# Norm shifts moved from VectorE to GpSimd, weight splitting moved from GpSimd to ScalarE and VectorE, and orders changed in a four-layer graph network

## Time and profile before

| | |
|---|---|
| median of three runs | 1450.76 us |
| the profiled execution, its own time | 1449.63 us |
| its span in the trace | 1447.8 us |
| TensorE busy | 1393.4 us, 96% |
| ScalarE busy | 1297.7 us, 90% |
| VectorE busy | 1235.4 us, 85% |
| GpSimd busy | 973.2 us, 67% |
| data moved | 39.74 MB, mean 27 GB/s |

### The profile page before, as it was taken

How to read it: one execution, slowest core, us unless ns; L and a number is a source line. 1 busy time by engine, 2 the same in 40 slices (tenths; PEclk the granted TensorE clock), 3 DMA queues, 4 the chain that set the end, 5 groups by cost and what they waited for, 6 DMA issues and landing times.

```text
span 1447.8 us, 45196 instructions
## 1 busy us (share of the span) xinstructions
PE 1393.4 (96%) x14088; PEld 1321.1 (91%) x14088; DVE 1235.4 (85%) x5648; ACT 1297.7 (90%) x4166; POOL 973.2 (67%) x1299
## 2 busy tenths in 40 slices
PE   5899999999999999999999999999999999999996
PEld 4799999999999999999999999999999999999985
DVE  3788889889889888888888888898898898898885
ACT  4899999999999999999999999999999999999973
POOL 4567667667667667667667667667667667667652
PEclk9999999999999999999999999999999999999998
DMA  3000000100001000101000001000101000101000
GB/s 113 17 17 16 24 21 26 31 20 28 31 19 29 31 18 31 31 17 31 31 17 31 31 17 31 31 17 31 31 17 31 31 17 31 31 16 38 16 23 31
DMA packets 38109, 39.74 MB, mean 27 GB/s; under 512 B 2416, under 2 KB 37488, under 8 KB 37872
## 3 DMA queue, kind: packets, MB, share of 16 engines
q1 hardware_dynamic: 37872, 36.84, 8.4%
HBM read 20.05 MB, written 16.78 MB: 25 GB/s over the span
## 4 chain that ended last, share of the span: by engine, by line
POOL 40%; DVE 30%; issue 20%; PE 7%; ACT 2%; SPq 1%; DVEq 0%; POOLq 0%; DMA 0%; ACTq 0%
DVE masked L751 10%; POOL rstd L952 7%; POOL h_t_lo L972 7%; DVE stats L741 6%; POOL probs L979 4%; POOL probs L1010 4%; POOL probs L960 4%; POOL probs L976 4%; POOL inv_norm L965 3%; POOL xb L1008 3%; PE mid L321 3%; DVE shift L814 3%; DVE y_t_lo L806 2%; POOL rel_sq L1004 2%; DVE neg_max L751 2%
## 5 line engine op out<-in xcount | busy, mean ns | idle before, releaser
L562 ACT ACTIVATE probs<-masked,neg_max 128x128 f32<-128x128 f32 x1024 | 396.7, 396 | 0.0
L952 POOL TENSOR_TENSOR rstd<-var_eps,minus_half 128x2 f32<-128x2 f32 x320 | 245.2, 766 | 25.1
L751 DVE CUSTOM_DVE_ANT_0 masked<-mid,mask 128x128 f32<-128x128 f32 x1024 | 234.0, 283 | 2.3 <-issue 2.2
L1004 POOL TENSOR_TENSOR rel_sq<-rel 128x256 f32<-128x256 f32 x64 | 39.3, 613 | 264.2 <-DVE rel L844 264.2
L562 ACT ACTIVATION_READ_ACCUMULATOR probs<-masked,neg_max 128x1 f32 x1024 | 200.1, 195 | 0.0
L356 PE MATMUL bank<-ident,probs 128*128 128x128 f32 x1024 | 143.4, 273 | 0.5 <-POOL probs L979 0.5
L741 DVE BATCH_NORM_STATS2 stats<-x 128x6 f32<-128x256 f32 x384 | 138.8, 403 | 3.8 <-DMA x<-in_x 3.5
L766 DVE SCALAR_TENSOR_TENSOR h_t_lo<-bank,h_t_hi 128x512 fp32r<-128x512 f32 x64 | 44.3, 691 | 105.3 <-ACT h_t_hi L644 105.3
L356 PEld LDWEIGHTS bank<-ident,probs 128*128 128x128 f32 x1024 | 115.9, 141 | 1.3 <-POOL probs L979 0.8
L644 ACT ACTIVATE h_t_hi<-bank 128x512 fp32r<-128x512 f32 x64 | 38.2, 597 | 80.0 <-PE mid L321 78.7
L972 POOL TENSOR_TENSOR h_t_lo<-h_t_full,h_t_hi 128x512 fp32r<-128x512 f32 x64 | 108.1, 1689 | 0.8 <-ACT h_t_full L660 0.8
(11 more groups left out here) (160 smaller groups left out, 5991.2 us busy)
## 6 DMA issues: line engine op xcount, KB each, us to landing
x<-in_x SPq DMA_DIRECT2D x64, 256.0 KB, 3.0
out_x<-x SPq DMA_DIRECT2D x64, 256.0 KB, 3.2
w_qkv_sb<-in_w_qkv SPq DMA_DIRECT2D x1, 768.0 KB, 5.0
w_v_sb<-in_w_v_t SPq DMA_DIRECT2D x1, 256.0 KB, 5.3
w_proj_sb<-in_w_proj SPq DMA_DIRECT2D x1, 256.0 KB, 5.5
w_q_sb<-in_w_q SPq DMA_DIRECT2D x1, 256.0 KB, 6.1
w_k_sb<-in_w_k SPq DMA_DIRECT2D x1, 256.0 KB, 6.5
w_gat_x<-in_w_gat SPq DMA_DIRECT2D x1, 256.0 KB, 6.1
```

Source lines behind the costliest of these rows:

```text
L562: last = act.activation(probs[:, r, s], masked[:, r, s], ACT.Exp, scale=-1.0, bias=neg_max[:, r, s:s + 1], accum_out=sums[:, r, s:s + 1])
L751: last = dve.tensor_tensor_reduce(out=masked[:, r, s], in0=mid[:, r, s * N:(s + 1) * N], in1=mask[:], scale=1.0, scalar=LARGE, op0=ALU.add ...
L952: pool.tensor_tensor(rstd[:, k], var_eps[:, k], minus_half[:], ALU.pow).then_inc(ln_rstd[k], 1)
```

## The change

1. All four shifts leave VectorE. GpSimd makes them right after rstd, in `inverse_root_and_shift`: it first makes the negated mean (one more 128x2 operation) and then the product (another).
2. The hi parts of `SPLIT` and `LATE_SPLIT` are made by ScalarE (start of its steps 1 and 2), the lo parts by VectorE (start of its steps 2 and 3). GpSimd keeps only the two sums of biases.
3. The fold moves from step 2 to step 3 on TensorE and ScalarE, its low part on VectorE from step 3 to 4; VectorE's `last_constants` (with beta_ident and wa_prod) from step 2 to 3.
4. On ScalarE the copy of v1 moves from between the exponentials of groups 3 and 2 to between h_t_hi of norm 0 (L644) and h_t_hi of norm 2 (L648).
5. On VectorE the inverse of the sums of groups 2 and 3 moves behind x4, and x3_up waits also for an earlier h3.

The diff, cut to its core:

```diff
@@ pe @@
             def fold():
-                pe.wait_ge(max_ready[0], done(0, 1))
+                pe.wait_ge(max_ready[0], done(1, 1))
...
             def next_weights():
-                pe.wait_ge(split_ready, 2 * len(SPLIT))
+                pe.wait_ge(split_lo_ready, len(SPLIT))
...
-            run(pe, step, [(0, first_weights), (1, value_weights), (2, fold), (4, folded_weights),
+            run(pe, step, [(0, first_weights), (1, value_weights), (3, fold), (4, folded_weights),
                           (2, next_weights), (6, last_weights)])
@@ act @@
+            def next_constants():
+                act.wait_ge(const_in, 16 * len(CONSTS))
+                for w, (hi, _) in SPLIT:
+                    act.activation(hi[:], w, ACT.Copy).then_inc(split_ready, 1)
+
+            def last_constants():
+                act.wait_ge(late_const_in, 16 * len(LATE_CONSTS))
+                for w, (hi, _) in LATE_SPLIT:
+                    act.activation(hi[:], w, ACT.Copy).then_inc(late_split_ready, 1)
...
                     exps(3).then_inc(probs_ready[3], 1)
-                if on[4]:
-                    act.wait_ge(v1_psum, done(p4))
-                    wait_before(act, rel_v_psum, p4)
-                    act.activation(v1[:].rearrange("p b d -> p (b d)"), v1_bank, ACT.Copy).then_inc(v1_ready, 1)
-                if on[1]:
                     act.wait_ge(max_ready[2], done(p1))
...
                     act.activation(flat(h_t[0][0]), z0_bank, ACT.Relu).then_inc(h_hi_ready[0], 1)
+                if on[4]:
+                    act.wait_ge(v1_psum, done(p4))
+                    wait_before(act, rel_v_psum, p4)
+                    act.activation(v1[:].rearrange("p b d -> p (b d)"), v1_bank, ACT.Copy).then_inc(v1_ready, 1)
                 if on[5]:
                     act.wait_ge(h_t_psum[2], done(p5))
...
-            run(act, step, [(0, first_weights), (2, copy_fold)])
+            run(act, step, [(0, first_weights), (3, copy_fold), (1, next_constants), (2, last_constants)])
@@ dve @@
             def next_constants():
                 dve.wait_ge(const_in, 16 * len(CONSTS))
+                for j, (w, (hi, lo)) in enumerate(SPLIT):
+                    dve.wait_ge(split_ready, j + 1)
+                    dve.tensor_tensor(lo[:], w, hi[:].bitcast(f32), ALU.subtract).then_inc(split_lo_ready, 1)
 
             def last_constants():
                 dve.wait_ge(late_const_in, 16 * len(LATE_CONSTS))
+                for j, (w, (hi, lo)) in enumerate(LATE_SPLIT):
+                    dve.wait_ge(late_split_ready, j + 1)
+                    dve.tensor_tensor(lo[:], w, hi[:].bitcast(f32), ALU.subtract).then_inc(late_split_lo_ready, 1)
...
+            moments_read = [shift_ready[0], shift_ready[1], shift_ready[2], shift3_ready, ln_rstd[4]]
+
             def moments(k, p, src):
-                wait_before(dve, ln_rstd[k], p)
+                wait_before(dve, moments_read[k], p)
...
-                if on[6]:
-                    dve.wait_ge(ln_rstd[2], done(p6))
-                    wait_before(dve, z_ready[2], p6)
-                    dve.scalar_tensor_tensor(shift[2][:], mean_var[:, 2, :, 0], -1.0, rstd[:, 2], ALU.mult, ALU.mult)\
-                       .then_inc(shift_ready[2], 1)
...
-            run(dve, step, [(1, first_constants), (3, fold_low), (2, next_constants), (2, last_constants)])
+            run(dve, step, [(1, first_constants), (4, fold_low), (2, next_constants), (3, last_constants)])
@@ pool @@
             def last_constants():
...
-                for w, (hi, _) in LATE_SPLIT:
-                    pool.tensor_copy(hi[:], w).then_inc(late_split_ready, 1)
-                pool.wait_ge(late_split_ready, len(LATE_SPLIT))
-                for w, (hi, lo) in LATE_SPLIT:
-                    pool.tensor_tensor(lo[:], w, hi[:].bitcast(f32), ALU.subtract).then_inc(late_split_ready, 1)
...
+            def inverse_root_and_shift(k, p, shift_k):
+                pool.wait_ge(ln_moments[k], done(p, 2))
+                pool.tensor_tensor(var_eps[:, k], mean_var[:, k, :, 1], eps[:], ALU.add).then_inc(ln_eps[k], 1)
+                pool.tensor_tensor(neg_mean[:, k], mean_var[:, k, :, 0], minus_one[:], ALU.mult).then_inc(ln_neg_mean[k], 1)
+                pool.wait_ge(ln_eps[k], done(p))
+                pool.tensor_tensor(rstd[:, k], var_eps[:, k], minus_half[:], ALU.pow).then_inc(ln_rstd[k], 1)
+                pool.wait_ge(ln_neg_mean[k], done(p))
+                pool.wait_ge(ln_rstd[k], done(p))
+                return pool.tensor_tensor(shift_k[:], neg_mean[:, k], rstd[:, k], ALU.mult)
...
                 if on[0]:
                     wait_before(pool, z_ready[0], p0)
-                    inverse_root(0, p0)
+                    inverse_root_and_shift(0, p0, shift[0]).then_inc(shift_ready[0], 1)
```

More of the change, by code:

```diff
@@ L81, in gnn_stack @@
         eps = sb("eps", [128, 2])
+        minus_one = sb("minus_one", [128, 2])
         turn = sb("turn", [1, 1])
@@ L99, in gnn_stack @@
         rstd = sb("rstd", [128, NORMS, 2])
+        neg_mean = sb("neg_mean", [128, NORMS, 2])
         shift = [sb(f"shift{k}", [128, 2]) for k in range(3)]
@@ L181, in gnn_stack @@
         sums_made, beta_made, wa_made = sem("sums_made"), sem("beta_made"), sem("wa_made")
+        split_lo_ready, late_split_lo_ready = sem("split_lo_ready"), sem("late_split_lo_ready")
         w_hi_ready, w_lo_ready, split_ready = sem("w_hi_ready"), sem("w_lo_ready"), sem("split_ready")
         ln_stats, ln_moments = sems("ln_stats", NORMS), sems("ln_moments", NORMS)
+        ln_neg_mean = sems("ln_neg_mean", NORMS)
         ln_eps, ln_rstd = sems("ln_eps", NORMS), sems("ln_rstd", NORMS)
@@ L383, in first_weights @@
             def first_weights():
-                pe.wait_ge(fills_made, 3)
+                pe.wait_ge(fills_made, 4)
                 pe.wait_ge(w_lo_ready, 2)
@@ L403, in next_weights @@
                 pe.wait_ge(const_in, 16 * len(CONSTS))
-                pe.wait_ge(split_ready, 2 * len(SPLIT))
+                pe.wait_ge(split_lo_ready, len(SPLIT))
             def last_weights():
                 pe.wait_ge(late_const_in, 16 * len(LATE_CONSTS))
-                pe.wait_ge(late_split_ready, 2 * len(LATE_SPLIT))
+                pe.wait_ge(late_split_lo_ready, len(LATE_SPLIT))
                 pe.wait_ge(wa_made, 2 * C + 2)
@@ L453, in step @@
                 if on[1]:
-                    if t == 2:
+                    if t == 3:
                         pe.wait_ge(folded_ready, 2)
@@ L779, in step @@
                     dve.wait_ge(x2_exp_ready, done(p8))
+                    wait_two_before(dve, h3_ready, p8)
                     dve.scalar_tensor_tensor(x3_up[:, i8], pair_rows(u_bank), 0.0, x2_exp[:], ALU.max, ALU.add)\
@@ L788, in step @@
                                                  ALU.mult, ALU.add).then_inc(x1_ready, 1)
[L789 to L793, removed]
                 if on[8]:
@@ L810, in step @@
                     least_masked(3).then_inc(max_ready[3], 1)
-                if on[6]:
-                    dve.wait_ge(ln_rstd[2], done(p6))
-                    wait_before(dve, z_ready[2], p6)
-                    dve.scalar_tensor_tensor(shift[2][:], mean_var[:, 2, :, 0], -1.0, rstd[:, 2], ALU.mult, ALU.mult)\
-                       .then_inc(shift_ready[2], 1)
-                if on[2]:
                     dve.wait_ge(scores_psum, done(p2))
@@ L845, in step @@
                        .then_inc(rel_ready, 1)
[L846 to L850, removed]
                 if on[3]:
@@ L854, in step @@
                     dve.tensor_tensor(o_res[:], pair_rows(o_bank), xb[:], ALU.add).then_inc(o_res_ready, 1)
[L855 to L860, removed]
                     dve.wait_ge(o_psum, done(p3))
                     dve.tensor_tensor(o[:], pair_rows(o_bank), both(b_proj_bc), ALU.add).then_inc(o_ready, 1)
[L863 to L866, removed]
                 if on[9]:
@@ L872, in step @@
                     dve.tensor_tensor(x4[:, i9], pair_rows(y_bank), x3b[:], ALU.add).then_inc(x4_ready, 1)
+                if on[2]:
+                    dve.wait_ge(probs_ready[2], done(p2))
+                    dve.wait_ge(probs_ready[3], done(p2))
+                    dve.reciprocal(inv_sums[:, 2:4], sums[:, 2:4]).then_inc(inv_sums_ready[1], 1)
                 if on[1]:
@@ L920, in _ @@
             pool.memset(eps[:], EPS).then_inc(fills_made, 1)
+            pool.memset(minus_one[:], -1.0).then_inc(fills_made, 1)
             pool.wait_ge(idents_zeroed, len(IDENTS))
@@ L924, in _ @@
                                    pattern=[[-1, 128]], channel_multiplier=1).then_inc(ident_made, 1)
-            pool.wait_ge(fills_made, 3)
+            pool.wait_ge(fills_made, 4)
             def next_constants():
@@ L929, in next_constants @@
                 pool.tensor_tensor(b_proj_beta[:], b_proj_bc[:], beta_ln_bc[:], ALU.add).then_inc(sums_made, 1)
[L930 to L934, removed]
                 pool.wait_ge(sums_made, 1)
```

(6 more changed lines are left out.)

## The result

The changed kernel takes 1456.3 us (median of five runs, 1454.07 to 1456.96) against 1450.57 us before (five runs on the same chip): ratio 1.0043, interval 1.0029 to 1.0057.

A forecast was written before the change was run, and what follows sets the result against it. One loop of ScalarE (10.20 us) and TensorE (11.58 us) was taken to bound the kernel. 57 x (0.48 - 0.11) = +21.1, start -1.0 and ends +0.8 gave +20.9 on 1449.6; forecast 1471 us, range 1460 to 1484.

The forecast's parts named there:

- The v1 copy, +0.48 a step: ScalarE between L644 and L450: the moved copy delays everything up to L578 by 0.48 us; bounds 0 and 0.60.
- The shifts, -0.11 a step with bounds 0 and -0.11: VectorE without the shifts: o_t_lo about 1 us sooner, removing TensorE's 0.11 us wait before the projection.
- at most 0.25 us a step can be won: TensorE in the middle steps: busy 213.50 of 216 us, so at most 0.25 us a step to win.
- VectorE is no link of the loop except through o_t_lo: Steady steps: VectorE affects the loop of ScalarE and TensorE only through o_t_lo, worth -0.11 us a step.
- a loop whose sum is the step (10.20 + 11.58): ScalarE from L644 to L450, 10.20 us, then TensorE to the next value product, 11.58 us: 21.78, the step.
- The collision, 0 on top: x_exp falls behind GpSimd's L972 and x2 comes 1.4 us later; counted as 0, upper bound 0.3 us.
- Rival C: Slower still: the late x_exp chain ends last, adding up to 0.3 us a step, 1475 to 1488 us; chance 0.12.
- GpSimd, 0.5 us a norm, hidden: GpSimd's added mean and shift: about 0.5 us a norm (bounds 0.2, 0.6), covered by its 4.3 us wait before rel_sq.
- Start and ends, -1.0 and +0.8: Start: moved fold and preparation, -1.0 us (bounds -4, +2); steps 4 to 6 and last steps: moved copy, +0.8 (0, 2).
- Rival A: Faster: the copy is absorbed in ScalarE's stretch and only the gains remain, 1435 to 1443 us; chance 0.07.
- D's time: A part of the loss: 0.15 to 0.3 us a step, 1457 to 1466 us; chance 0.07.
- L454's wait of 0.3 to 0.6 us: TensorE ahead of the y_t product (old L450): waits for ScalarE's L578 some 0.3 to 0.6 us each.

The follow-up runs named there:

- e4: e1 with ScalarE's copy of group 2's probabilities moved ahead of the copy of k_t; 1406.63 us, ratio 0.9707 to the kernel before.
- e6: The kernel before with only ScalarE's copy of group 2's probabilities moved ahead of that of k_t; 1449.67 us (one run), step 21.77 us.
- e2: The kernel before with only the v1 copy moved behind h_t_hi of norm 0; 1523.1 us (one run), step 23.03 us.
- e5: e2 with ScalarE's u_exp two copies earlier, ahead of h_t_hi of norm 1; 1462.01 us (one run), step 21.90 us at the median.
- e1: The changed kernel with only the v1 copy put back between the exponentials of groups 3 and 2; 1428.28 us, ratio 0.9852 to the kernel before.
- e3: The kernel before with norm 2's shift still on VectorE but moved behind o_t_lo; 1437.15 us, ratio 0.9906.

## Why the prediction was wrong in size

The direction was right, and so were the mechanism and the price of the moved copy. One term of the sum was wrong, the gain from the shifts, and so was the picture of the loops that it came from.

- **The v1 copy, +0.48 a step.** Right: h_t_hi to L454 is 10.69 us, the figure forecast, with ScalarE busy throughout and the copy at h_t_hi + 0.49.
- **The shifts, -0.11 a step with bounds 0 and -0.11.** This is the step that failed. Measured -0.39. I took the wait for o_t_lo from the difference of length and busy time (11.58 - 11.47), that is from modelled ends of matmuls, and made this the bound too. For the same reason "at most 0.25 us a step can be won" was wrong: e4's step is 0.72 us shorter. From start to start the gap was 1.16 against 0.81 us. A second row, of the weight loads, had 0.28 and I didn't read it. 57 x 0.28, the error of this term (0.39 - 0.11), is 16 us, and the forecast was 15 too high: the step is 21.88 us, not 22.14.
- **"VectorE is no link of the loop except through o_t_lo".** The sentence hid the larger mistake: through o_t_lo VectorE closed a loop of its own, of 21.78 us, and that one set the step. I had found a loop whose sum is the step (10.20 + 11.58) and stopped. Its second part contained the wait that belongs to the other loop, so the sum had to come out right. e6 shows it: L450 starts 0.31 us sooner and nothing is won.
- **The collision, 0 on top.** x_exp takes 1.46 us after, near the 1.39 of the last steps, and VectorE, freed of the shifts, hides it. Timelines of VectorE and GpSimd, after:

```profile
700.57 1.46 DVE L893 SCALAR_TENSOR_TENSOR x_exp<-u_exp,x 128x512 f32<-128x512 f32 x1 [0.89 <-ACT u_exp L677]
```
```profile
700.20 1.28 POOL L974 TENSOR_TENSOR h_t_lo<-h_t_full,h_t_hi 128x512 fp32r<-128x512 f32 x1
```

Rival C priced the effect of this at up to 0.3 us with some 0.3 of cover; in the changed kernel it cost nothing, in e2, where the shifts stay on VectorE, 0.78. The rule of the Trainium skill (SBUF — State Buffer, section "SBUF: two separate sides"), by which the one of the two that starts second is blocked until the first is done, agrees with the 1.46 and 1.47 us: x_exp, begun second, ends 0.55 us behind GpSimd's instruction in both (702.03 and 701.48; 713.65 and 713.10), not quite the 0.69 that it takes when it runs by itself.
- **GpSimd, 0.5 us a norm, hidden.** 0.36 us, inside the bounds, and without effect on the step: 2.0 us of its wait ahead of rel_sq are left. The 0.26 us that VectorE waits for e_mask I hadn't counted; VectorE's loop has room for it (21.58 against 21.88).
- **Start and ends, -1.0 and +0.8.** Measured, from ScalarE's second h_t_hi on: -0.79 and -0.81 in steps 2 and 3, +0.45 and +0.69 in steps 6 and 7, -0.61 behind step 64. A further -1.2 lies ahead of the second h_t_hi; the same mark stands between 24.6 and 27.5 us in the nine experiments, whatever their edits.
- **Rival A** (the copy is absorbed) was wrong as put, since nothing in ScalarE's stretch gave way. D's time (1457 to 1466) was nearly met, by another way: the loss was whole and a larger gain stood against it.

Expected but not met: L454's wait of 0.3 to 0.6 us is 0.27 in TensorE's row, where again a part is hidden.

## What to carry to other kernels

Where engines go round in step, write down every loop, with its waits left out of each part, and take the longest; a loop whose parts were measured with another loop's wait inside always sums to the step and proves nothing. Measure a wait of TensorE from start to start against the same group where it doesn't wait, not from its busy time. And price an instruction on an in-order engine by where it stands: the same 0.48 us copy was free at one place, and at another it cost 0.13 us in most steps (e5, together with the earlier u_exp), 0.48 (the change against e1) and 1.26 (e2), by what else was in the way.

## What the runs showed that I had not expected

- A 128x2 operation on VectorE, 0.15 us by itself, cost the kernel 0.35 us a step by its place, and VectorE's loop 0.94: it started during a 1.29 us GpSimd operation, ended with it and so took 1.03 us, and stood ahead of o_t_lo. e3 won this back by moving it behind o_t_lo.
- One copied tensor 0.48 us later made a neighbouring operation 0.78 us longer (e2): it slipped from 0.11 us ahead of GpSimd's instruction to 0.37 behind it. The order of the two starts decided which of them grew: when VectorE was first, GpSimd's instruction grew by 0.44 (1.29 to 1.73).
